# A convolution-attention and motif kernel: the feature rows of the terms' first two slabs loaded at the end of the gram stage, into one shared buffer

## The reference

```python
x = x + _L0_conv_ref(_gn(x), ...)     # 1x1 and depthwise 3x3 convolutions, 4-head channel attention, 1x1 convolution
x = x + _L1_conv_ref(_gn(x))          # motif terms, with [B, C, H, W] read as (2, 128, 128, 96)
```

```python
gram = einsum('bgjcl,bgjdl->bgjcd', motif, motif)        # 9 shifted views of 8 planes per group
nn_idx = argmin(d2, axis=-1);  u_max = max(nn_idx);  c_max = sum(nn_idx == u_max)
motif_nn = take_along_axis(motif, u_max)                 # one neighbour view per group and shift
term = floor(motif * motif_nn * c_max / Cg)
out[:, :, :, ki:ki+Hm, kj:kj+Wm] += (motif * batch_mask + term)   # for the nine shifts k
```

## Time and profile before

| | us |
|---|---|
| median of 3 runs | 1478.48 |
| lowest, highest | 1476.63, 1479.1 |
| span of the profiled execution | 1473.2 |
| mean granted TensorE clock in it | 0.956 |

### The profile page before, as it was taken

How to read it: one execution, slowest core, us unless ns; L and a number is a source line. 1 busy time by engine, 2 the same in 40 slices (tenths; PEclk the granted TensorE clock), 3 DMA queues, 4 the chain that set the end, 5 groups by cost and what they waited for, 6 DMA issues and landing times. The chain is left out here.

```text
span 1473.2 us, 34011 instructions
## 1 busy us (share of the span) xinstructions
PE 1317.6 (89%) x13586; PEld 1057.6 (72%) x13586; DVE 1140.7 (77%) x1896; ACT 887.0 (60%) x1013; POOL 656.8 (45%) x672
## 2 busy tenths in 40 slices
PE   3899998996899499999989999999959968999998
PEld 1789997996899355555548899879949954555554
DVE  6577777368873599999976777755887839999998
ACT  3566664211553299999965556532135508999996
POOL 4888894243220144534019888814412113444400
PEclk9999999898999699999999999999979978999999
DMA  5466631494215343553438866309405225274533
GB/s 212 125 190 195 204 108 52 121 315 139 88 52 208 140 146 92 160 132 111 119 104 245 250 207 187 84 19 281 123 1 216 109 91 184 78 188 108 147 72 103
DMA packets 75876, 210.27 MB, mean 143 GB/s; under 512 B 15306, under 2 KB 15414, under 8 KB 72646
## 3 DMA queue, kind: packets, MB, share of 16 engines
q1 hardware_dynamic: 61214, 158.10, 34.0%
q0 software_dynamic: 6720, 36.93, 9.3%
q10 hardware_dynamic: 7784, 13.07, 3.3%
HBM read 91.54 MB, written 67.04 MB: 108 GB/s over the span
## 5 line engine op out<-in xcount | busy, mean ns | idle before, releaser
L1771 PE MATMUL acc<-rnd,ident 128*128 128x376 f32 x1152 | 391.8, 484 | 15.9 <-ACT rnd L1748 15.9
L1771 PEld LDWEIGHTS acc<-rnd,ident 128*128 128x128 f32 x1152 | 217.0, 192 | 136.3 <-ACT rnd L1748 17.3
L956 PE MATMUL ps_a<-wa,xa 128*128 128x192 f16 x1536 | 296.2, 247 | 9.0 <-DMA xc<-low 6.9
L956 PE MATMUL ps_a<-wb,xb 128*128 128x192 f16 x1536 | 295.0, 246 | 0.0
L1743 ACT ACTIVATE rnd_m<-prod,plus_round,scale 128x1504 f32<-128x1504 f32 x144 | 235.8, 1637 | 43.1 <-DVE prod L1592 32.5
L574 POOL TENSOR_TENSOR vt<-z 96x256 f32<-96x256 f32 x248 | 254.7, 1047 | 4.2 <-ACT z L850 4.0
L1707 DVE SCALAR_TENSOR_TENSOR over<-prod,scale,rnd 128x1504 bf16<-128x1504 f32 x144 | 256.5, 1784 | 0.0
L1748 ACT ACTIVATE rnd<-rnd_m,minus_round 128x1504 f32<-128x1504 f32 x144 | 223.2, 1550 | 4.7
L1651 POOL DMA_INDIRECT near<-f_planes,index x42 | 122.8, 2923 | 146.2 <-DVE prod L1592 139.7
L956 PEld LDWEIGHTS ps_a<-wa,xa 128*128 128x128 f16 x1536 | 150.4, 98 | 12.3 <-DMA xc<-low 8.3
L956 PE MATMUL ps_a<-wfa,xa 128*128 128x96 f16 x1536 | 157.7, 207 | 1.7 <-issue 1.6
(11 more groups left out here) (338 smaller groups left out, 2468.8 us busy)
## 6 DMA issues: line engine op xcount, KB each, us to landing
xb<-xa ACTq DMA_DIRECT2D x64, 195.0 KB, 2.7
f_planes<-img SPq DMA_DIRECT2D x8, 1536.0 KB, 13.9
fc<-f_planes SPq DMA_DIRECT2D x16, 768.0 KB, 5.7
v_a<-xa SPq DMA_DIRECT2D x40, 260.0 KB, 2.6
v_b<-xb SPq DMA_DIRECT2D x40, 260.0 KB, 3.1
xa<-v_a SPq DMA_DIRECT2D x40, 260.0 KB, 4.4
xb<-v_b SPq DMA_DIRECT2D x40, 260.0 KB, 5.1
v_c<-xc SPq DMA_DIRECT2D x40, 195.0 KB, 3.4
```

Of the source, the lines that this page charges most:

```text
L956: mm = lambda a, w, first, end: nc.tensor.matmul(out(i), a, w, start=first, stop=end)
L1771: nc.tensor.matmul(o(m), k["ident"][:, :], rnd[:, n % RNDS, BR * m:BR * m + BR, :], start=False, stop=False, skip_group_check=True)
```

## The change

One buffer `shared` of 12 x 1040 half-precision numbers a partition is allocated in `build` and lives through the program. In attention it holds `xa`, in the grams `turned_hi[0]`, `g_all` and `both`, in the terms `fc`; these had allocations of their own. The first two loads of `fc` move from the head of SP's queue in the terms to the tail of its queue in the grams, behind the waits for the stores and a new wait for three finished chunks. They count on a semaphore of their own, `fc_ahead`, which products 0 and 1 wait for; the other slabs' loads stay where they were, and their counts are adapted. The two loads cover 3072 single-precision numbers a partition from the start of the buffer, which is within `turned_hi[0]`; `g_all` and `both` lie behind that.

```diff
-        xa = sb("xa", [P, SLOTS, 8, PADW], F16)
+        xa = shared[:, 0:SLOTS * SLOT].rearrange("p (s i x) -> p s i x", s=SLOTS, i=8)
...
-        turned_hi = [sb(f"turned_hi{s}_", [P, TCOLS + 8], F16) for s in range(2)]
+        turned_hi = [shared[:, 0:TCOLS + 8], sb("turned_hi1_", [P, TCOLS + 8], F16)]
...
-        g_all = sb("g_all", [MR, MG, MR], F32)
+        after_turned = (TCOLS + 8) // 2
+        g_all = (shared[:].bitcast(F32)[0:MR, after_turned:after_turned + MG * MR]
+                 .rearrange("p (g r) -> p g r", g=MG))
...
             sp.wait_ge(f_out, 16 * NQ)
+            sp.wait_ge(chunk_done, 3)
+            fc = shared[:].bitcast(F32)[:, 0:2 * SLAB * C].rearrange("p (s e) -> p s e", s=2)
+            for i in range(2):
+                sp.dma_start(fc[:, i, :], f_dram[:, SLAB * i * C:SLAB * (i + 1) * C]).then_inc(fc_ahead, 16)
...
-        fc = sb("fc", [P, SLOTS, R * C], F32)
+        fc = shared[:].bitcast(F32)[:, 0:SLOTS * R * C].rearrange("p (s e) -> p s e", s=SLOTS)
...
-                eng.wait_ge(fc_in[s], 16 * (i // SLOTS + 1))
+                if i < 2:
+                    eng.wait_ge(fc_ahead, 32 * (b + 1))
+                else:
+                    eng.wait_ge(fc_in[s], 16 * ((i - 2) // SLOTS + 1))
...
-            for i in range(2):
-                load_rows(fc, f_dram, i, fc_in)
...
+        fc_ahead = ctx.enter_context(nc.semaphore("fc_ahead"))
+        shared = sb("shared", [P, SLOTS * SLOT], F16)
```

More of the change, by code:

```diff
@@ L411, with attention @@
        "dup_in0", "dup_in1", "dup_in2")
-def attention(nc, b, k, x, img, v_dram, x1_rows, x1_out, sems):
+def attention(nc, b, k, x, img, shared, v_dram, x1_rows, x1_out, sems):
     UNITS = H // 4
@@ L1080, with motif_grams @@
              "pick_pe", "grams_out2", "next_in", "next_stats", "lo_first", "sum_done", "sum_out0", "sum_out1")
-def motif_grams(nc, b, k, img, x_after, f_dram, x1_rows, x1_out, att_sems, sems):
+def motif_grams(nc, b, k, img, shared, fc_ahead, x_after, f_dram, x1_rows, x1_out, att_sems, sems):
     CHUNK = 24
@@ L1124, in motif_grams @@
         block_picks = sb("block_picks", [MG, 3, KK], F32)
-        both = sb("both", [P, 2, 3, KK], F32)
+        after_all = after_turned + MG * MR
+        both = (shared[:].bitcast(F32)[:, after_all:after_all + 6 * KK]
+                .rearrange("p (h v j) -> p h v j", h=2, v=3))
         bank = [ctx.enter_context(nc.psum_tensor(f"ps_m{j}_{b}", [P, 512], F32)) for j in range(8)]
@@ L1514, in _, with motif_terms @@
             c.then_wait(nc.vector.tensor_reduce(k["pick"][:], both[:], X, ALU.add))
-def motif_terms(nc, b, k, x, room, f_dram, out, gram_sems, att_sems):
+def motif_terms(nc, b, k, x, room, shared, fc_ahead, f_dram, out, gram_sems, att_sems):
     R = SLAB
@@ L1815, in build @@
         for b in range(B):
-            attention(nc, b, k, x, img, v_dram[b], x1_rows[b], x1_out, att_sems)
-            motif_grams(nc, b, k, img, x[b + 1] if b + 1 < B else None, f_dram[b], x1_rows[b], x1_out, att_sems,
+            attention(nc, b, k, x, img, shared, v_dram[b], x1_rows[b], x1_out, att_sems)
+            motif_grams(nc, b, k, img, shared, fc_ahead, x[b + 1] if b + 1 < B else None, f_dram[b], x1_rows[b], x1_out, att_sems,
                         gram_sems)
@@ L1820, in build @@
             img = held.enter_context(nc.sbuf_tensor(f"img{b + 1}", [P, H, C], F32)) if b + 1 < B else None
-            motif_terms(nc, b, k, x, img, f_dram[b], out, gram_sems, att_sems)
+            motif_terms(nc, b, k, x, img, shared, fc_ahead, f_dram[b], out, gram_sems, att_sems)
 _INS = ["x", "L0_conv_w_qkv", "L0_conv_b_qkv", "L0_conv_w_dw", "L0_conv_b_dw", "L0_conv_temperature",
```

## The result

The first measurement gave 1469.31 us (median of 4 runs, 1466.73 to 1473.19) for the changed kernel beside 1478.09 us (4 runs) for the one before: a ratio of 0.9935, interval 0.9916 to 0.9954. Longer measurements then gave less. Timed twice more beside the kernel before, the change had ratios of 0.9963 (interval 0.9937 to 0.9988) and 0.9974 (0.9943 to 1.0005). Over these two, the means are 1470.95 us (24 runs) and 1475.76 us (58 runs), 4.8 us apart. The kernel before ran between 1466.56 and 1487.6 us in these 58 runs; the four that it was first judged by (1476.63 to 1479.1) showed neither its middle nor its spread.

A forecast was written before the change was run, and what follows sets the result against it. The terms were taken as bound by when VectorE's loop of products and overshoots starts, set by product 2's wait for the row move. Gains 4.7 + 2.6 = 7.3 us: span 1465.9, plus 5.3 to the median, 1471.2 us; range 1469.3 to 1475.2.

The forecast's parts named there:

- The price of a byte: Start of the terms: loads and gathers share DMA engines at 0.407 MB/us; removing the two loads' 1.573 MB saves 3.86 us.
- The check: Image 0 before the change: all bytes plus the fixed time put the third gather at 510.19; the move went at 510.21.
- the fixed part: A gather's time beyond issue and bytes, from a lone 0.442 MB gather in the trace: 1.85 us.
- The signs: Expected in the changed profile: product 2 about 4 us behind product 0 in image 0, about 6.4 in image 1.
- Image 1, 2.6 us: Start of image 1's terms: third gather lands at 1217.40 instead of 1219.98, product 2 starts at 1219.9; gain 2.6 us.
- Image 0, 4.7 us: Start of image 0's terms: move goes at about 507.1, takes 2.3 us; product 2 at 509.5 instead of 514.22.
- VectorE's moments: Image 0: VectorE works on the next image's moments until 505.28, so product 0 is made only at 507.0, after the gather.
- Rival A: First move of image 0 again takes 4.0 us; image 0 gains 3.1, sum 5.7, time 1472.8; chance 0.22.
- Rival B: TensorE at its lower clock makes VectorE wait 3.2 us at image 0's overshoot 3; sum 4.1, time 1474.4; chance 0.12.
- Rival C: The software queue runs no faster with free engines; third gather lands as now, nothing gained, 1478.5; chance 0.08.
- Rival D: Attention matmuls reading xa at its new place cost more, at 5 ns each 15.4 us, time 1486.6; chance 0.04.
- Nothing for the early loads: Two loads at the grams' end on SP cost nothing, covered by 55 and 27 us of empty queue.

The follow-up runs named there:

- its two variants of layout: Kernel before with near2 and fc allocations exchanged, and kernel before with an unused 64-byte buffer ahead of the image: first moves 4.1 us, image 0 heads 17.9 and 18.1.

## Why the prediction was right and wrong

The direction and the chain were right. The heads in the middle of all profiles of each kind (four of the kernel before, with its two variants of layout, three of the changed one) are 17.9 and 14.8 us before and 14.3 and 13.8 after: 3.6 us in image 0 and 1.0 in image 1, 4.6 in all. 4.7, 2.6 and 7.3 were forecast.

*The price of a byte.* This is the step that failed: the size of one term, and with it the overlap that the term ignores. The third gather was to land at 498.45 + 1.85 + 6.03 in image 0 and at 1217.40 in image 1, 9.85 and 9.7 us behind the start. It came at 11.8 and 11.3 in the middle. The term "2.455 MB at 0.407 MB/us, 6.03 us" was mis-sized; by the landings it was about 7.8 us, some 315 GB/s. Nearly all of the excess lies between the first landing and the second. So the removed 1.573 MB, priced at 3.86 us, were worth 1.9 us in image 0 and 0.9 in image 1; the rest had filled time in which the gathers alone do not use the engines. The check that seemed to confirm the model, 510.19 against 510.21, could not do so: with both loads in the mix the engines were full, and the model had never been tried where they were not. The lone gather of the earlier trace rows gave the fixed part rightly: the first gather was expected 4.9 us after its issue and landed at 5.1. The signs show the same: product 2 came 5.3 us behind product 0 in image 0 and 8.2 in image 1, where about 4 and 6.4 were foreseen.

*Image 1, 2.6 us.* It was 1.0. The forecast's chain of events held (the third gather still the last to come, the move 2.6 us), only the landing moved less.

*Image 0, 4.7 us.* It was 3.6. The third gather did not come before product 0 was made, so the bound "VectorE's moments" never came into play: the move went at 11.8 us and not at 10.6. The sum also counted as gained the slow move's 4.0 against 2.3, and that part came true (2.3 to 2.5), but not because the median of all moves is typical of this place. The bytes of the loads gave 1.9 us (16.2 to 14.3, the shared buffer with the loads at the head against the changed kernel). The other 1.7 (17.9 to 16.2) are the row that waited behind the instruction packet: without the loads the move's rows are through at 13.7 to 14.1 us, before that packet begins. The forecast took this part as gained without knowing what had held the move, so it is luck. The buffer was costed at nothing, and no run shows that it gained or cost anything by itself.

*Rival A*, the first move slow again, did not happen in any of the three profiles. The rival was right that bytes were not the reason, but its reading of the rows was not: the bytes after 513.5 in the earlier trace rows are slab 1's move. What held the first one was, by the packets' times, a packet at a fixed place of TensorE's program, and that the change would bring the move ahead of it I had not thought of.

*Rival B*, TensorE's clock: overshoot 3 began at 518.45, 11.63 us behind product 2 as before, without a wait. It fell.

*Rival C*, the gathers' own pace, fell for the first gather (5.1 us instead of 7.3) and was half right for the third, which came 0.9 us earlier in image 1 where 2.6 were forecast. A case between the two, a freed DMA engine that is not fully used, should have had most of the chance.

*Rival D*, xa's new place: matmuls that read `xa` in the shared buffer take 247 ns, as before. It fell.

*Nothing for the early loads.* They went at 459.1 and 1179.0, and the barrier did not wait for SP; grams took 126 to 129 us in both kernels.

*The range.* It took the spread of the runs from three values (1476.63 to 1479.1) and allowed 1 us for it. The kernel before scatters by 5.2 us (standard deviation), and medians of four runs of each kernel can be 9 us apart where 4.6 are due. The first measurement's 9 us and its interval (6.8 to 12.4 us) were such a case: the time fell below the range by the scatter of the runs, while the mechanism gave less than forecast. The 5.3 us between the profiled span and the median, which the forecast keeps, are in part scatter too: within one execution time and span are 1.8 us apart (1469.96 and 1468.2 for the changed kernel).

## What to carry to other kernels

Ask of a transfer that is to be moved away not how many bytes it has, but whether the DMA engines would be full without it: its neighbours' rate must be read at the place and moment at which they will be alone. A model with one free rate that fits the crowded case says nothing about the empty one; one run with more load and one with less would have shown the bend. When a transfer is late without bytes to move, look at which other queue's packets its engines carried before the layout is blamed. And before a fraction of a percent is explained, cut several profiles of the same kernel at the same events: here the part that the change touches repeats within 0.7 us, while stages that it does not touch scatter by 9.

## What the runs showed of the hardware

- Four gathers of 0.79 to 0.88 MB on one software queue move 166, 393, 303 and 228 GB/s in their first four microseconds and 417 to 425 from 1213 to 1215; when 1.57 MB of loads from another queue go first, the engines move 178 and then 412 to 424. A first load of 0.79 MB beside the gathers costs the third of them 0 to 0.4 us, a second 0.5 to 1.8, a third 1.6 to 2.0.
- A row move of 0.10 MB inside the buffers takes 2.3 to 2.8 us when it is issued with one gather still under way and 2.7 to 4.9 with two; it is through 0.2 to 0.4 us behind the last gather.
- One packet of 16 KB on the instruction queue takes 1.0 to 1.5 us on its DMA engine. In the five profiles in which a row or a completion of the first move waits until that packet is through, the whole move takes 3.5 to 4.1 us instead of 2.3 to 3.2. That they share an engine is argued from the times.
- The same stretch of attention (260 to 280 us) has a mean granted clock of 1.00 in nine profiles and 0.66 in five; attention 0 takes 362 to 365 us with the first and 367 to 371 with the second.
